# Sixteen of thirty sums over the feature dimension moved from VectorE to ScalarE in 16-column pieces, with new scheduling tables

## The reference

```
e  = stack(tbl_f[ids[:, f]] for f in 32 fields)                 # [512, 32, 16]
xk = e
for W in (W0, W1, W2):                                          # 32x32x64, 32x64x64, 32x64x64
    xk = relu(einsum('bmd,bhd,mhk->bkd', e, xk, W))             # [512, 64, 16]
    z += [sum(xk, axis=2)]                                      # [512, 64], the sums of this document
h = relu(concat(z, dense_ctx) @ W_top1 + b_top1)                # 208 -> 512
h = relu(h @ W_top2 + b_top2)                                   # 512 -> 256
y = h @ W_top3                                                  # [512, 1]
```

## Time and profile before

| | |
|---|---|
| median of 3 runs | 339.63 us |
| span of the profiled execution, first to last instruction | 356.2 us |
| TensorE busy | 314.8 us (88%) |
| VectorE busy | 282.1 us (79%), 172 instructions |
| GpSimd busy | 246.0 us (69%), 195 instructions |
| ScalarE busy | 53.3 us (15%), 77 instructions |
| the 30 sums on VectorE | 17.1 us |

### The profile page before, as it was taken

The page is one execution under the profiler, slowest core; times in us unless marked ns, Lnnn a source line. Parts: engine busy times, 40 slices in busy tenths (PEclk is TensorE's granted clock), DMA queues, the critical chain, the costliest instruction groups (busy, mean ns, idle before and its releaser), DMA issues.

```text
span 356.2 us, 4290 instructions
## 1 busy us (share of the span) xinstructions
PE 314.8 (88%) x1602; PEld 114.9 (32%) x1602; DVE 282.1 (79%) x172; ACT 53.3 (15%) x77; POOL 246.0 (69%) x195
## 2 busy tenths in 40 slices
PE   0378588988699788898999999998999999999997
PEld 0344224432222223332333333332333333333334
DVE  0039477869499878999999999999998879999220
ACT  1000011012020221110112120121022111220011
POOL 5646566766367668869997987896998569729300
PEclk9999989999899999999999999999999999999999
DMA  6272853834875982979499989683699897050000
GB/s 183 65 231 72 230 154 73 230 71 110 295 240 174 326 292 65 326 217 280 167 317 289 296 284 297 201 268 67 215 346 337 290 291 194 17 133 2 0 0 0
DMA packets 34302, 68.09 MB, mean 191 GB/s; under 512 B 5866, under 2 KB 15082, under 8 KB 34282
## 3 DMA queue, kind: packets, MB, share of 16 engines
q1 hardware_dynamic: 23562, 56.80, 49.0%
q10 hardware_dynamic: 6624, 9.96, 9.4%
q0 software_dynamic: 4096, 1.06, 3.5%
HBM read 55.55 MB, written 2.03 MB: 162 GB/s over the span
## 4 chain that ended last, share of the span: by engine, by line
PE 59%; POOL 16%; issue 11%; DVE 9%; another core or an unknown queue 2%; DMA 1%; DVEq 1%; ACT 0%; POOLq 0%; SPq 0%
PE acc L1060 37%; PE acc L1055 12%; POOL gathered L719 10%; DVE vz L805 8%; POOL pz L746 6%; PE factor L984 2%; PE factor L1093 2%; PE factor L1021 1%; PE factor L1088 1%; PE acc L1050 1%; PE factor L998 1%; PE acc L1082 1%; PE factor L1100 1%; DVEq L800 1%
## 5 line engine op out<-in xcount | busy, mean ns | idle before, releaser
L805 DVE TENSOR_TENSOR vz<-fields_sb,factor 128x1024 f32<-128x1024 f32 (+3 forms) x113 | 230.5, 2090 | 20.7 <-PE factor L984 7.6
L1060 PE MATMUL acc<-vz,w_sb 128*64 128x512 f32 (+1 forms) x800 | 172.6, 569 | 10.9 <-DVE vz L805 3.6
L719 POOL DMA_INDIRECT gathered<-in_table,index x128 | 121.6, 950 | 65.0 <-issue 31.5
L746 POOL TENSOR_TENSOR pz<-fields_sb,hidden 128x1024 f32<-128x1024 f32 (+1 forms) x52 | 117.9, 2292 | 19.4 <-DMA hidden<-relu_out 9.6
L1060 PEld LDWEIGHTS acc<-vz,w_sb 128*64 128x64 f32 x800 | 57.8, 139 | 113.7 <-issue 98.6
L1055 PE MATMUL acc<-vz,w_sb 128*64 128x512 f32 x216 | 60.9, 621 | 3.7 <-DVE vz L805 2.9
L1060 PE MATMUL acc<-pz,w_sb 128*64 128x512 f32 x192 | 48.1, 594 | 0.3 <-POOL pz L746 0.3
L934 ACT ACTIVATE relu_out<-acc 128x512 f32<-128x512 f32 (+1 forms) x30 | 15.3, 512 | 126.3 <-PE acc L1060 47.3
L890 ACT ACTIVATE factor<-hidden 128x1024 f32<-128x1024 f32 (+1 forms) x23 | 20.1, 878 | 65.8 <-DMA hidden<-relu_out 34.3
L805 DVE TENSOR_TENSOR vz<-rotated,factor 128x2048 f32<-128x2048 f32 x12 | 26.9, 2279 | 1.8 <-issue 1.8
L1055 PEld LDWEIGHTS acc<-vz,w_sb 128*64 128x64 f32 x216 | 16.4, 139 | 36.4 <-issue 24.6
(11 more groups left out here) (44 smaller groups left out, 83.2 us busy)
## 6 DMA issues: line engine op xcount, KB each, us to landing
fields_sb<-fields SPq DMA_DIRECT2D x48, 512.0 KB
rotated<-fields SPq DMA_DIRECT2D x24, 512.0 KB
fields_sb<-fields SPq DMA_DIRECT2D x32, 256.0 KB
hidden<-relu_out ACTq DMA_DIRECT2D x30, 256.0 KB, 5.6
own<-fields SPq DMA_DIRECT2D x6, 512.0 KB
gathered<-in_table,index POOLq DMA_INDIRECT x128
hidden<-relu_out ACTq DMA_DIRECT2D x16, 128.0 KB
fields<-gathered SPq DMA_DIRECT2D x6, 256.0 KB, 5.2
```

Of the source, the lines that this page charges most:

```text
L719: nc.gpsimd.indirect_dma_start(gathered[:, pair % GRING, j, :], None, table, bass.IndirectOffsetOnAxis(ap=index[:, i:i + 1], axis=0)).then ...
L746: nc.gpsimd.tensor_tensor(pz[:, at % PRING, 0:cols], fields[s][:, t, col:col + cols], hidden_of(step, g), ALU.mult).then_inc(pz_ready, 1)
L805: nc.vector.tensor_tensor(vz[:, at:at + nt, 0:cols].rearrange("p t (a n) -> p t a n", n=half), src[:, t:t + nt, col:col + cols].rearrange( ...
L1060: last = nc.tensor.matmul(acc_of(step, ab), w_sb[layer][:, kt, :], z[:, ab * half:(ab + 1) * half], start=start and j == 0, stop=stop and ...
```

## The change

Sixteen steps' sums are made by ScalarE: a copy of 16 columns of `relu_out` at a time into a tile that nobody reads, with its sum over those columns as accumulator output, one value per row, 32 pieces for a wide step and 16 for a narrow one. They stand in ScalarE's queue in two parts, one and two wide tiles behind the relu's due place. The other fourteen stay on VectorE. A second semaphore, `sums_done_act`, counts them, and whoever waited for `sums_done` waits for the one or the other.

With it the tables BEGUN, SPREAD (5 steps to 4), HALF (7 to 10), POOL_TILES (52 tiles to 49), FIRST_GATHERS (21 to 26), GATHERS_IN, PACED, BEHIND_SPREAD (13 entries to 6), PAIRED (7 steps to 2) and LOADS are new.

```diff
+SUMS_ON_ACT = [(0, 0), (1, 1), (1, 2), (2, 1), (1, 3), (2, 2), (0, 4), (2, 3), (1, 4), (1, 5), (0, 6), (2, 4),
+    (2, 5), (0, 7), (1, 6), (1, 7)]
+SUMS_LAG, SUMS_PARTS = PAIR, 2
-SPREAD = [(1, 0), (2, 3), (1, 4), (1, 5), (1, 9)]
-HALF = [(2, 0), (1, 2), (2, 2), (1, 3), (2, 4), (1, 7), (2, 7)]
-POOL_TILES = {(1, 0): 0, (2, 0): 0, (1, 1): 1, (2, 1): 0, (1, 2): 0, (2, 2): 0, (1, 3): 0, (2, 3): 3, (1, 4): 1,
-    (1, 5): 5, (2, 4): 3, (2, 5): 4, (1, 6): 4, (1, 7): 3, (2, 6): 4, (2, 7): 5, (1, 8): 6, (1, 9): 4, (2, 8): 3,
-    (2, 9): 6}
-FIRST_GATHERS = 21
+SPREAD = [(1, 0), (2, 2), (1, 4), (1, 8)]
+HALF = [(2, 0), (1, 1), (1, 2), (1, 3), (2, 3), (1, 5), (2, 4), (2, 5), (1, 7), (1, 9)]
+POOL_TILES = {(1, 0): 0, (2, 0): 0, (1, 1): 0, (2, 1): 0, (1, 2): 0, (2, 2): 0, (1, 3): 0, (2, 3): 2, (1, 4):
+    3, (1, 5): 3, (2, 4): 4, (2, 5): 4, (1, 6): 4, (1, 7): 2, (2, 6): 4, (2, 7): 4, (1, 8): 5, (1, 9): 6, (2,
+    8): 4, (2, 9): 4}
+FIRST_GATHERS = 26
...
-PAIRED = [(2, 0), (1, 1), (1, 2), (2, 1), (2, 2), (1, 3), (2, 3)]
+PAIRED = [(1, 2), (2, 1)]
...
+BY_VECTOR = [step for step in ORDER if step not in SUMS_ON_ACT]
+BY_SCALAR = [step for step in ORDER if step in SUMS_ON_ACT]
...
-    places, due = {}, list(ORDER)
+    places, due = {}, list(BY_VECTOR)
...
+        if step in SUMS_ON_ACT:
+            for part in range(SUMS_PARTS):
+                due.append((COLUMNS[vectors_to(step)] + (JOIN_LAG if step in PAIRED else 0) + RELU_LAG + (1 + part) * SUMS_LAG,
+                            "sums", step, part))
...
-                    act.wait_ge(sums_done, n - RRING + 1)
+                    summed(act, [before])
...
+            def act_sums(step, part):
+
+                layer, b = step
+                pair, col, cols, _, _ = BLOCKS[b]
+                first, count = col // DIM // 2, cols // DIM // 2 // SUMS_PARTS
+                if not part:
+                    act.wait_ge(relu_done, ORDER.index(step) + 1)
+                    if BY_SCALAR.index(step):
+                        act.wait_ge(sums_done_act, BY_SCALAR.index(step))
+                for j in range(part * count, (part + 1) * count):
+                    last = nc.scalar.activation(unread[:, j * DIM:(j + 1) * DIM], relu_of(step)[:, j * DIM:(j + 1) * DIM], ACT.Copy,
+                                                accum_out=feats[layer][:, pair, first + j:first + j + 1])
+                if part == SUMS_PARTS - 1:
+                    last.then_inc(sums_done_act, 1)
```

More of the change, by code:

```diff
@@ L58, in turn @@
     return sum(1 for a in range(b) if stream(a) == stream(b))
-BEGUN = [(0, 0), (1, 0), (0, 1), (2, 0), (0, 2), (1, 1), (0, 3), (1, 2), (2, 1), (2, 2), (1, 3), (0, 4), (0, 5),
-    (2, 3), (1, 4), (1, 5), (2, 4), (0, 6), (2, 5), (0, 7), (1, 6), (1, 7), (0, 8), (2, 6), (2, 7), (0, 9), (1,
-    8), (1, 9), (2, 8), (2, 9)]
+BEGUN = [(0, 0), (1, 0), (0, 1), (2, 0), (0, 2), (1, 1), (0, 3), (1, 2), (2, 1), (1, 3), (2, 2), (0, 4), (0,
+    5), (2, 3), (1, 4), (1, 5), (0, 6), (2, 4), (2, 5), (0, 7), (1, 6), (1, 7), (2, 6), (0, 8), (2, 7), (0,
+    9), (1, 8), (1, 9), (2, 8), (2, 9)]
@@ L84 @@
-FIRST_GATHERS = 21
[L85 to L90, removed]
[5 rows of a table removed]
-BEHIND_SPREAD = {10: 1, 11: 3, 15: 4, 24: 5, 26: 6, 36: 7, 43: 8, 45: 9, 55: 10, 61: 11, 80: 12, 85: 13, 93: 14}
+SPREAD = [(1, 0), (2, 2), (1, 4), (1, 8)]
@@ new lines @@
+HALF = [(2, 0), (1, 1), (1, 2), (1, 3), (2, 3), (1, 5), (2, 4), (2, 5), (1, 7), (1, 9)]
[3 more added lines that the diff above has]
+FIRST_GATHERS = 26
+GATHERS_IN = {(0, 1): (1,), (0, 2): (9,), (0, 3): (4,), (0, 4): (27,), (0, 5): (16,), (2, 3): (1, 1), (1, 4):
+    (6, 0, 0), (1, 5): (5, 1, 0), (2, 4): (1, 4, 0, 0), (2, 5): (1, 3, 0, 2), (1, 6): (3, 0, 0, 1), (1, 7):
+    (4, 6), (2, 6): (2, 0, 0, 4)}
@@ L100 @@
+PACED = {11: 1, 14: 2, 16: 2, 17: 4, 18: 4, 19: 6, 21: 8, 22: 9, 24: 9, 26: 12, 27: 14, 29: 15, 31: 17, 32:
[5 rows of a table added]
+BEHIND_SPREAD = {36: 3, 38: 3, 74: 3, 88: 3, 109: 3, 123: 8}
 AFTER_ROW = (8,)
-PAIRED = [(2, 0), (1, 1), (1, 2), (2, 1), (2, 2), (1, 3), (2, 3)]
+PAIRED = [(1, 2), (2, 1)]
 TURN_LEAD, TURN_STEP = 4, 1
@@ L120 @@
 LOADS = [('scratch', 0), ('fields', 0), ('scratch', 1), ('operands', 1), ('fields', 1), ('scratch', 2),
[L121 to L124, removed]
+    ('scratch', 3), ('operands', 2), ('operands', 3), ('fields', 2), ('fields', 3), ('scratch', 4),
+    ('operands', 4), ('scratch', 5), ('operands', 5), ('fields', 4), ('scratch', 6), ('fields', 5),
+    ('operands', 6), ('scratch', 7), ('operands', 7), ('fields', 6), ('fields', 7), ('scratch', 8),
+    ('operands', 8), ('scratch', 9), ('operands', 9), ('fields', 8), ('fields', 9)]
 OWN, ACROSS = -1, L0TILES
@@ L390, in scalar_program @@
                 due.append((max(free, first - OWN_LEAD), "put", step, g))
-    relus = [item for item in due if item[1] in ("fold", "relu")]
+    relus = [item for item in due if item[1] in ("fold", "relu", "sums")]
     puts, late = sorted((item for item in due if item not in relus), key=lambda item: FACTORS.index(item[2:])), 0
@@ L404 @@
 assert [step for what, step, g in SCALAR if what == "copy"] == COPIED
+assert [step for what, step, g in SCALAR if what == "sums" and not g] == BY_SCALAR
+for _n in range(RRING, len(ORDER)):
+    if ORDER[_n - RRING] in SUMS_ON_ACT:
+        assert SCALAR.index(["sums", ORDER[_n - RRING], SUMS_PARTS - 1]) < SCALAR.index(["relu", ORDER[_n], 0])
 def cin_dlrm(nc, table, ids, first_row, unit, pairs, turned, across, w0a, w0b, w0c, w1, w2, wt1, bt1, wt2,
@@ L439, in cin_dlrm @@
         folds = sb("folds", [P, N])
+        unread = sb("unread", [P, N])
         turned_sb = sb("turned_sb", [P, L0TILES, P])
@@ L483, in cin_dlrm @@
         folded, joined = sem("folded"), sem("joined")
-        relu_done, sums_done = sem("relu_done"), sem("sums_done")
+        relu_done, sums_done, sums_done_act = sem("relu_done"), sem("sums_done"), sem("sums_done_act")
         relayed = {(step, g): sem(f"relayed{step[0]}_{step[1]}_{g}") for step in BEGUN
@@ L547, in relayed_halves, with summed @@
             return [1] if step in HALF else range(HHALF)
+        def summed(engine, steps):
+            for order, done in ((BY_VECTOR, sums_done), (BY_SCALAR, sums_done_act)):
+                count = max([order.index(step) + 1 for step in steps if step in order], default=0)
+                if count:
+                    engine.wait_ge(done, count)
         def pools_read(step):
@@ L672, in _ @@
             for layer in range(2):
-                sp.wait_ge(sums_done, ORDER.index((layer, LAST)) + 1)
+                summed(sp, [(layer, b) for b in range(len(BLOCKS))])
                 for ab in range(2):
@@ L955, in _ @@
                     copy_hidden(step, g)
+                elif what == "sums":
+                    act_sums(step, g)
                 elif what == "fold":
@@ L1133, in _ @@
             top1_first(1)
-            pe.wait_ge(sums_done, len(ORDER))
+            summed(pe, ORDER)
             for ab in range(2):
```

## The result

The changed kernel takes 342.39 us (median of 4 runs, 342.15 to 342.77), the kernel before on the same chip 339.54 (4 runs, 339.0 to 340.64). The ratio is 1.0091, interval [1.0063, 1.0119]: 2.9 us slower, where 336.0 was forecast. The profiled execution has a span of 340.3 us and a time of 342.15 of its own.

The account below looks back on a forecast made before the run. VectorE was taken to bound the kernel before 198.7 us, TensorE at its rate after. Terms -3.7 - 0.5 + 0.6 = -3.6 us gave 352.6 profiled, 336.0 us unprofiled; range 331 to 347, the forecast's own 333 to 338.

Parts of the forecast that it names:

- The price of a piece: ScalarE's cost per 16-column sum: 0.20 us taken, bounds 0.085 and 0.364, 80 us for all 400.
- The border at 198.7 us: From there TensorE runs at its rate; only VectorE work removed before it was to bring a gain.
- the 16.6 us between span and median: Profiled span 356.2 us against unprofiled median 339.63; subtracted from the forecast span of 352.6 us.
- The relief, -3.7 us: Reductions leaving VectorE before 198.7 us: 4.7 us, less 1 us for six narrow ones from 18 to 101 us.
- Rival B: No change, 339 us: GpSimd or the operands' DMAs set the pace before 198.7 us; chance 0.18.
- The delays, +0.6 us: ScalarE's relus, relays and puts standing behind pieces come later, including (1,1)'s put and relu in the narrow steps: +0.6 us.
- full but passable: ScalarE from 153 to 249.9 us: 89 of 97 us at 0.20 us a piece, full at 0.23.
- TensorE's next need for that bank is a whole step away: At a layer-0 step behind a wide one, the relu up to 5 us late was to be harmless.
- The cover of 3 us: After the relay of (1,6): pieces end 1.4 us past a put's time, inside the 3 us VectorE leaves.
- The tables, -0.5 us and 0: Five fewer folds and joins: -0.5 us, bounds 0 and 7.3; VectorE's tile moves and the gather order: 0 each.
- Rival A: Slower, 346 us: a piece costs over 0.23 us, ScalarE's queue fills from about 160 us; chance 0.27.

Follow-up runs that it names:

- sums left out: Kernel before's tables, one ScalarE copy of 16 or 32 columns replacing each moved sum: 338.5 us, 0.9978; same edit on the changed kernel: 340.8 us, 1.0012.
- early eight: Sums (0,0), (1,1), (1,2), (2,1), (1,3), (2,2), (0,4), (2,3); only these moved, kernel before's tables: 338.55 us, 0.9968; new tables: 339.09 us, 0.9994.
- late eight: Sums (1,4), (1,5), (0,6), (2,4), (2,5), (0,7), (1,6), (1,7); only these moved to ScalarE, kernel before's tables: 345.74 us, 1.0183.
- two kernels with 96 pieces in the wide steps: Kernel before's tables, early eight moved, plus (1,4), (2,5), (0,7) in ScalarE's gaps: 339.22 us, 0.9991; or (1,5), (0,6), (1,6) before puts: 343.5 us, 1.0124.
- the kernel with three before puts: Kernel before's tables, early eight moved, plus (1,5), (0,6), (1,6) between relay DMAs and the next layer-0 put: 343.5 us, 1.0124.
- the second profile of before: The kernel before, unchanged, profiled once more: one run, 339.81 us, with a span of 338.0 us.
- three kernels with the new tables and no late pieces: Changed kernel with all sums on VectorE, 340.33 us; with sixteen sums left out, 340.8 us; with the late eight back on VectorE, 339.09 us.

## Why the prediction was wrong

**The price of a piece: right.** 0.20 us was taken as "two overlapped operations of small size", and so it is: an ACTIVATE of 200 ns and an ACTIVATION_READ_ACCUMULATOR of 186 ns, about 0.10 us each from start to start (32 pieces of two instructions take 6.37 us, from 191.62 to 197.99, so 0.199 each). ScalarE's busy time came to 127.8 us against "near 130", VectorE's to 277.1 against "274 to 278". The term called the weakest held.

The Trainium skill (ScalarE: Activation LUTs, What ACT_TABLE_LOAD costs) gives figures for an ACTIVATE from which an estimate of a piece is 0.106 us. The trace agrees for that instruction (about 0.10 us to the next start) and shows a second of nearly the same length behind it, so about twice the estimate.

**The border at 198.7 us, from which on TensorE is at its rate: wrong, and the first failed step.** It was read from an execution 18.2 us longer than the second one. The warning stood in my own sum: the 16.6 us between span and median, which I subtracted with the words that the profile does not show where they lie. They lay ahead of 250 us, in the very stages from which the gain was to come. In the two later profiles the span lies 1.8 and 1.9 us below the execution's time. From 150 us on, TensorE is at its rate, so by my own reading sums removed there are worth nothing; and before 101 us VectorE's idle time is half of what I read. **The relief, -3.7 us, measures -0.7 us** under the old tables (-1.5 to 0.0, sums left out) and -0.2, give or take 1.1, under the new ones (1.0012 beside 1.0019). The early eight, with their pieces on ScalarE, measure -1.1 and -0.8. Rival B had the size, but not the cause from 150 us on, where neither GpSimd nor DMAs but TensorE itself sets the pace. Before that, what share the operands' DMAs have wasn't tried.

**The delays, +0.6 us: wrong, and the second failed step, which turned the sign.** The late eight alone measure +3.3 us in the changed kernel. I asked whether ScalarE's queue gets full, found that it would be at 0.23 us a piece, and called 0.20 "full but passable". That holds, and it was the wrong question: ScalarE works through its queue in order, and a run of 32 pieces delays whatever stands behind it by up to 6.4 us, whether the queue is full or not. The two kernels with 96 pieces in the wide steps show it: 0.9991 and 1.0124 at 48 and 47 us of ScalarE in 170.

Two sentences of that step can be looked at singly. "TensorE's next need for that bank is a whole step away" thought of the bank only: TensorE also reads a relu's output, for the spread of the next layer, and at 198.61 it waits 0.79 us for the relu behind the pieces to do so. The cover of 3 us for "1.4 us past the put's time" was measured at one put of one trace, that of (2,6), and taken for all. At that put the changed kernel's trace doesn't decide, since the relay's DMA may have been late as well; at the put of (0,8), 7 us later than without pieces, VectorE idles 1.11 us, and in the kernel with three before puts 3.97 us at the put of (0,6).

**The tables, -0.5 us and 0: small, as said, but not of the forecast sign.** They measure +0.6 us (-0.1 to +1.4). Fewer folds and joins brought nothing that shows; they were not tried apart from the other tables, so why stays open.

**Rival A.** Its signature came, VectorE behind puts and TensorE behind relus between 150 and 270 us, but not its condition: a piece costs less than 0.23 us, and the queue isn't full (ScalarE is busy 73.93 of 170 us). I had tied the right effect to the wrong condition. The range of 331 to 347 us holds the measured time only because it leaves room for this rival, and slower runs had a chance of 0.28. The kernels under the new tables split the whole change: the tables +0.6 us, the early eight moved -0.8 (1.0019 to 0.9994, give or take 1.1), the late eight moved +3.3 (0.9994 to 1.0091), together 3.1; measured are 2.9 to 3.1 with an interval of 2.1 to 4.0.

**What stays open.** The way from the pieces to GpSimd's two late products at 217.82 and 238.58, 1.48 us of TensorE's 3.60. How much of the 2.37 us at the put of (2,6) is the relay's DMA. And whether TensorE's clock is what the new tables cost. From 18 to 101 us the granted clock is 0.94 to 0.96 in all five profiles under the new tables and 0.98 in the eight under the old ones (the first, long one has 0.96). In the second profile of before it falls to 0.50 (1.2 GHz) once, from 28 to 31 us; in the changed kernel it does so a second time, from 55 to 58, behind two microseconds (53 to 55) in which TensorE was busy for 0.01 us. Of the 36 executions of the three kernels with the new tables and no late pieces, the 8 with a mean clock of 0.995 took 338.7 us on average, the 16 with 0.990 took 340.1 and the 12 with 0.985 took 340.9. The four of the changed kernel show no such order. No run changed the clock alone.

## What to carry to other kernels

Before work is moved to an idle engine that runs in order, list what stands behind it in that engine's queue and when the busiest engine needs each of these; the free time that counts here was the one ahead of the next relu or put, not the free share of the stretch. A wait that appears in the changed kernel's trace is not yet its price: look for the same wait in a kernel without the added work, as two of the five here were. Work taken off an engine counts only where that engine ends the wait: if TensorE is already without a hole, sparing VectorE brings nothing. And when the span of a profile is 5% off the times of the runs, take a second profile before any border between stages is read from it.

## What the hardware showed that I had not expected

- An ACTIVATE with an accumulator output is two instructions in the trace. For 128x16 they last 200 and 186 ns, overlap to about 0.10 us each, and come to 0.20 us a piece; 32 pieces, the 512 columns that VectorE sums in 0.68 us, take 6.4 us.
- Two profiled executions of one kernel had spans of 356.2 and 338.0 us at mean granted clocks of 0.990 and 0.995, so TensorE's clock explains little of the 18.2 us between them. All of it had arisen by 250 us; why the first was longer wasn't tried.
